# A head's values as high and low parts in one stationary block of the attention stages

## The reference

```python
# layer 0: 16 heads of 32, causal
q, k, v = ((x @ W.T).reshape(B, T, 16, 32).transpose(0, 2, 1, 3) for W in (Wq, Wk, Wv))
w = softmax(einsum('bhtd,bhsd->bhts', q, k) / sqrt(32) + mask)
z = einsum('bhts,bhsd->bhtd', w, v)
out = z.transpose(0, 2, 1, 3).reshape(B, T, 512) @ Wo.T
# layer 1: 32 query heads of 64 in 8 groups (4 query heads share one k and one v), causal
y = rms_norm(x) ; q, k, v = split(y @ w_in.T) ; q, k = rope(q), rope(k)
attn = softmax(where(causal, einsum('bghsd,bgxpd->bghsp', q, k) * 64 ** -0.5, -inf))
o = einsum('bghsp,bgxpd->bghsd', attn, v)
out = x + o.transpose(0, 3, 1, 2, 4).reshape(B, T, 2048) @ w_out.T
```

## Time and profile before

| | us |
|---|---|
| median of 3 runs | 2130.75 |
| the three runs | 2122.9, 2130.75, 2133.69 |
| the profiled execution | 2136.04 |
| its span, first to last instruction | 2134.7 |

### The profile page before, as it was taken

The page is one execution under the profiler, slowest core; times in us unless marked ns, Lnnn a source line. Parts: engine busy times, 40 slices in busy tenths (PEclk is TensorE's granted clock), DMA queues, the critical chain, the costliest instruction groups (busy, mean ns, idle before and its releaser), DMA issues. The chain is left out here.

```text
span 2134.7 us, 30662 instructions
## 1 busy us (share of the span) xinstructions
PE 1889.3 (89%) x10274; PEld 1632.2 (76%) x10274; DVE 1129.9 (53%) x2767; ACT 788.8 (37%) x2029; POOL 967.3 (45%) x926
## 2 busy tenths in 40 slices
PE   5788979878999999899569999999998999897896
PEld 4676867657899898799447888888877788785795
DVE  4555685437333333235746666666665656455344
ACT  2554643231222222121146556565553423212231
POOL 2332341248782759813736546455453101006584
PEclk8899999999999999899789999999999999789998
DMA  2434531025663446431533333233321110002565
GB/s 88 134 110 137 159 135 67 1 88 203 230 203 120 154 161 220 157 118 51 157 77 91 85 85 101 60 89 83 79 66 46 60 45 1 20 1 96 174 205 195
DMA packets 102630, 232.33 MB, mean 109 GB/s; under 512 B 18752, under 2 KB 19008, under 8 KB 99408
## 3 DMA queue, kind: packets, MB, share of 16 engines
q1 hardware_dynamic: 82736, 144.89, 22.8%
q0 software_dynamic: 19744, 85.47, 12.1%
HBM read 126.23 MB, written 57.93 MB: 86 GB/s over the span
## 5 line engine op out<-in xcount | busy, mean ns | idle before, releaser
L631 POOL TENSOR_SCALAR a_E<-a_E,a_inv 128x128 f32<-128x128 f32 (+3 forms) x384 | 218.9, 588 | 278.1 <-DVE a_inv L752 278.1
L149 PE MATMUL bank<-f_UH,f_XH 128*128 x596 | 202.2, 339 | 19.8 <-POOL f_UL L161 14.8
L664 ACT ACTIVATE a_E<-a_E,a_top 128x512 f32<-128x512 f32 (+3 forms) x384 | 211.1, 567 | 8.4 <-DVE a_top L746 8.3
L746 DVE CUSTOM_DVE_ANT_0 a_E<-a_causal,bank 128x512 f32<-128x512 bf16 (+3 forms) x384 | 164.2, 482 | 73.3 <-PE bank L897 45.9
L149 PE MATMUL bank<-f_UH,f_XL 128*128 x596 | 194.6, 327 | 0.0
L149 PE MATMUL bank<-f_UL,f_XH 128*128 x596 | 194.6, 326 | 0.0
L656 ACT ACTIVATE a_PHL<-bank 128x512 fp32r<-128x512 f32 (+1 forms) x288 | 131.2, 528 | 156.0 <-PE bank L913 156.0
L149 PE MATMUL bank<-a_PHL,a_VH 128*128 128x512 f32 (+3 forms) x768 | 186.7, 332 | 0.3 <-DVE a_QL L161 0.3
L161 DVE TENSOR_TENSOR a_PHL<-bank,a_PHL 128x512 fp32r<-128x512 f32 (+1 forms) x288 | 153.8, 587 | 29.7 <-ACT a_PHL L656 29.6
L1603 DVE TENSOR_TENSOR f_gate<-bank,f_gate 128x352 f32<-128x352 f32 x79 | 41.3, 523 | 215.9 <-PE bank L149 215.9
L149 PEld LDWEIGHTS bank<-a_PHL,a_VH 128*128 128x128 f32 x768 | 140.3, 196 | 16.3 <-DVE a_QL L161 0.6
(11 more groups left out here) (389 smaller groups left out, 4976.2 us busy)
## 6 DMA issues: line engine op xcount, KB each, us to landing
f_uraw<-f_up POOLq DMA_DIRECT2D x18, 1408.0 KB, 6.5
f_xb<-table SPq DMA_DIRECT2D x86, 256.0 KB, 3.1
table<-f_ob SPq DMA_DIRECT2D x86, 256.0 KB, 2.3
table<-a_zeros SPq DMA_DIRECT2D x31, 512.0 KB, 4.3
f_draw<-f_down POOLq DMA_DIRECT2D x27, 512.0 KB, 4.5
a_g<-a_f SPq DMA_DIRECT2D x160, 64.0 KB, 2.0
a_raw<-a_qkv SPq DMA_DIRECT2D x36, 256.0 KB, 3.1
f_uraw<-f_up POOLq DMA_DIRECT2D x9, 704.0 KB, 4.8
```

Of the source, the lines that this page charges most:

```text
L149: m = pe.matmul(out, a, b, start=first and i == 0 and j == 0, stop=last and i == n - 1 and j == 2, skip_group_check=not check)
L631: e.tensor_scalar(self.E[sl][:, a], self.E[sl][:, a], self.inv[:, sl, i:i + 1], 0.0, ALU.mult, ALU.add).then_inc(*self.s_nrm.up(N, m - 1, i))
L664: x = e.activation(E, E, ACT.Exp, scale=-1.0, bias=self.top[:, sl, i:i + 1], accum_out=self.total[:, sl, i:i + 1])
L746: e.tensor_tensor_reduce(self.E[sl][:, self.E_AT[i]:self.E_AT[i] + w], self.causal[:, T - w:T], bank[:, off:off + w], -1.0, HUGE, ALU.add, ...
```

## The change

- One block `V` of 128 x 128 per head and key tile takes the place of `VH` and `VL`: the high parts stay in the head's own columns, the low parts go to the columns 64 further on, modulo 128 (`across`).
- A job's weighted values are two matmuls for each key block and no longer three: `V` by the high weights and `V` by the low weights. The head's own rows get the high values' sum, the rows across get the low values' sum.
- Because the rows across are in use, only half of the heads share an accumulation (`half`): one head in a1, two in a0. So `bank[7]` is read out after every job in a1 (before: every second), and after every second job in a0 (before: every fourth), and the next group's first matmul waits for that readout.
- A readout is now: ScalarE copies 64 rows to `QH`; VectorE subtracts (64 rows), waits for its own result, and adds the rows across (`_dve_low_rows`).
- GpSimd clears one `V` in a0 and nothing of it in a1 (before: `VH` and `VL` in both).

```diff
@@ __init__
-        self.VH, self.VL = sb("VH", [heads, NT, P], F32R), sb("VL", [heads, NT, P], F32R)
+        self.V = sb("V", [heads, NT, P], F32R)
...
+        self.across = [slice((h * hd + P // 2) % P, (h * hd + P // 2) % P + hd) for h in range(heads)]
+        self.half = heads // 2
+        self.rows = [slice(0, P // 2), slice(P // 2, P)]
@@ pool
-        for z in (self.VH, self.VL):
-            e.memset(z[:, :, :, :].bitcast(F32), 0.0)
+        if self.heads > 2:
+            e.memset(self.V[:, :, :, :].bitcast(F32), 0.0)
@@ act
-            if 3 <= m < self.M + 3 and self.jobs[m - 3][3] == self.heads - 1:
+            if 3 <= m < self.M + 3 and self.jobs[m - 3][3] % self.half == self.half - 1:
                 j, b, r, h = self.jobs[m - 3]
+                own = self.rows[h // self.half]
                 e.wait_ge(*self.s_av.after(N, m - 3))
-                e.activation(self.QH[:, r, b * T:b * T + T], self.k.bank[self.OB][:, :], ACT.Copy).then_inc(
-                    *self.s_ohi.up(N, j, r, b))
+                e.activation(self.QH[own, r, b * T:b * T + T], self.k.bank[self.OB][own, :], ACT.Copy).then_inc(
+                    *self.s_ohi.up(N, j, r, b, h // self.half))
@@ dve
-            if 3 <= m < self.M + 3 and self.jobs[m - 3][3] == self.heads - 1:
...
+            if 3 <= m < self.M + 3 and self.jobs[m - 3][3] % self.half == self.half - 1:
+                self._dve_low_rows(*self.jobs[m - 3])
+
+    def _dve_low_rows(self, j, b, r, h):
+        e, N, g, bank = self.k.dve, self.name, h // self.half, self.k.bank[self.OB]
+        own, other = self.rows[g], self.rows[1 - g]
+        low = self.QL[own, r, b * T:b * T + T]
+        e.wait_ge(*self.s_ohi.after(N, j, r, b, g))
+        low_part(e, low, bank[own, :], self.QH[own, r, b * T:b * T + T]).then_inc(*self.k.d.up())
+        e.wait_ge(*self.k.d.now())
+        e.tensor_tensor(low, bank[other, :], low.bitcast(F32), ALU.add).then_inc(*self.s_olo.up(N, j, r, b, g))
@@ _dve_fill
-                    i = low_part(e, self.VL[:, h, bs, cs], src[:, :, cs], self.VH[:, h, bs, cs], scale=1.0)
+                    i = low_part(e, self.V[:, h, bs, self.across[h]], src[:, :, cs], self.V[:, h, bs, cs], scale=1.0)
@@ _pe_values
-        if h == 0 and self.OB in emptied:
+        first, last = h % self.half == 0, h % self.half == self.half - 1
+        if first and self.OB in emptied:
             e.wait_ge(*emptied[self.OB])
...
-                t = product(e, self.k.bank[self.OB][:, sblk * P:T],
-                            [(self.VH[:, h, b * TT + sblk, :], self.VL[:, h, b * TT + sblk, :])],
-                            [(self.PH[m % 2][:, a], self.PL[m % 2][:, a])],
-                            first=h == 0 and sblk == 0, last=h == self.heads - 1 and ci == 2)
+                e.matmul(out, self.V[:, h, at, :], self.PH[m % 2][:, a], start=first and sblk == 0, stop=False)
+                t = e.matmul(out, self.V[:, h, at, :], self.PL[m % 2][:, a], start=False, stop=last and ci == 2)
...
-        if h == self.heads - 1:
-            emptied[self.OB] = self.s_olo.after(N, j, r, b)
+        if last:
+            emptied[self.OB] = self.s_olo.after(N, j, r, b, h // self.half)
```

More of the change, by code:

```diff
@@ L531, in plan @@
                 self.s_av.plan((N, m))
-                if h == self.heads - 1:
-                    self.s_ohi.plan((N, j, r, b))
-                    self.s_olo.plan((N, j, r, b))
+                if h % self.half == self.half - 1:
+                    self.s_ohi.plan((N, j, r, b, h // self.half))
+                    self.s_olo.plan((N, j, r, b, h // self.half))
     def moves(self, j, c, b):
@@ L706, in _act_fill @@
                 e.wait_ge(*self.s_vt.after(N, j, b))
+                bs = slice(b * TT, b * TT + TT)
                 for h, cs in self.head_rows:
-                    i = e.activation(self.VH[:, h, b * TT:b * TT + TT, cs], src[:, :, cs], ACT.Copy, scale=1.0)
+                    i = e.activation(self.V[:, h, bs, cs], src[:, :, cs], ACT.Copy, scale=1.0)
                 i.then_inc(*self.s_vhi.up(N, j, b))
@@ L769, in dve @@
                 self.norm.dve_rest(NT + m)
-            if 3 <= m < self.M + 3 and self.jobs[m - 3][3] == self.heads - 1:
-                j, b, r, h = self.jobs[m - 3]
-                a = slice(b * T, b * T + T)
-                e.wait_ge(*self.s_ohi.after(N, j, r, b))
-                low_part(e, self.QL[:, r, a], self.k.bank[self.OB][:, :], self.QH[:, r, a]).then_inc(
-                    *self.s_olo.up(N, j, r, b))
+            if 3 <= m < self.M + 3 and self.jobs[m - 3][3] % self.half == self.half - 1:
[8 more added lines that the diff above has]
+        e.tensor_tensor(low, bank[other, :], low.bitcast(F32), ALU.add).then_inc(*self.s_olo.up(N, j, r, b, g))
     def _dve_rotate(self, x):
@@ L870, in _pe_fill @@
                 if g % TT == 0:
-                    e.wait_ge(*self.s_olo.after(N, j, self.queries[-1], g // TT))
+                    e.wait_ge(*self.s_olo.after(N, j, self.queries[-1], g // TT, 1))
                 a = slice(g * P, g * P + P)
@@ L928, in _pe_values @@
             for sblk, _ in chunk:
-                a = slice(self.P_AT[sblk], self.P_AT[sblk] + T - sblk * P)
-                t = product(e, self.k.bank[self.OB][:, sblk * P:T],
-                            [(self.VH[:, h, b * TT + sblk, :], self.VL[:, h, b * TT + sblk, :])],
-                            [(self.PH[m % 2][:, a], self.PL[m % 2][:, a])],
-                            first=h == 0 and sblk == 0, last=h == self.heads - 1 and ci == 2)
+                a, at = slice(self.P_AT[sblk], self.P_AT[sblk] + T - sblk * P), b * TT + sblk
+                out = self.k.bank[self.OB][:, sblk * P:T]
+                e.matmul(out, self.V[:, h, at, :], self.PH[m % 2][:, a], start=first and sblk == 0, stop=False)
+                t = e.matmul(out, self.V[:, h, at, :], self.PL[m % 2][:, a], start=False, stop=last and ci == 2)
         t.then_inc(*self.s_av.up(N, m))
-        if h == self.heads - 1:
-            emptied[self.OB] = self.s_olo.after(N, j, r, b)
+        if last:
+            emptied[self.OB] = self.s_olo.after(N, j, r, b, h // self.half)
     def end(self):
```

## The result

The changed kernel is slower by 0.7%: ratio 1.0071, 95% interval 1.0052 to 1.009; the medians of 10 runs each are 2144.15 us and 2127.03. The forecast was 2123. The profiled execution took 2146.57 us for 2136.04.

A forecast was written before the change was run, and what follows sets the result against it. Latency chains through ScalarE, SP, GpSimd and VectorE were taken to bound part of a1, TensorE the rest. a1 +2.6 and a0 -10.5 gave -7.9 us: 2128.1 profiled, 2123 median, 8-in-10 range 2104 to 2143.

The forecast's parts named there:

- The third pass: Values of each job: one of three passes saved, 0.63 us; 40 us in a1 and 20 in a0 if all on the path.
- a1, the stretch that TensorE sets: From B to the next projection before A: three V blocks saved and a small stall given back, -2.14 us per 8 jobs.
- B: Second of two a1 loops in eight (at 1376.96) beginning with scores waiting for stacking copies; wait 1.56 us, expected some 3.1.
- a1, loops without one before: a1 loops that had no readout: mask shifts about 1.7 us, hidden by VectorE's 1.94 us idle time at A, others similar.
- A: First of two a1 loops in eight (at 1360.84) beginning with scores waiting for stacking copies; wait 0.83 us, expected some 2.4.
- The clock: Longer waits drop TensorE's clock at B in all 8 groups instead of 4, 1.6 us each: +6.4 us in a1.
- a1, end: Last jobs of a1, without fill: each waits for the readout before it; +3.1 us, bounds -3.8 and +7.
- a1, start: Start of a1: GpSimd's two clearings go, so the norm on VectorE is faster; -1.5 us, bounds 0 and -2.9.
- a0: Stage a0: V blocks saved in loops that TensorE sets, little lost in the four end loops without fill; -10.5 us.
- VectorE becomes the bound: a1 loops without an earlier readout: shift over 1.94 us makes the rotation's first step late; +26 us, 2149 us, chance 0.16.
- Lighter chains: Sum of the rows across costs only 0.35 us, shortening chains before A and B, clock stays high: 2111 us, chance 0.20.
- "clock": Rival: all growing waits, one in a0 too, drop TensorE's clock; 6.4 us more, 2129 us, chance 0.15.

The follow-up runs named there:

- the copy first everywhere: Changed kernel with ScalarE's copy of the finished block ahead of its evacuation of a projection in all of a1: ratio 1.0057, a1 606.7 us.
- the waits filled: Changed kernel with identity matmuls on TensorE ahead of the scores' waits, 6 at A and 13 at B: ratio 1.0111, a1 613.6 us.
- the pass without its price: Kernel before, in a1 without the low values by high weights pass, still one readout per two jobs: ratio 0.9931, a1 571.6 us.

## Why the prediction was wrong

In the terms of the profiled execution I had -7.9 us and it was +10.5 (between the medians +17.1, of which the traces show only the 10.5). By its steps:

- **The third pass** was sized right (TensorE's loops without a wait went from 7.07 to 6.43 us, 0.64) and so was **the sum's own time** (0.69).
- **"a1, the stretch that TensorE sets"**: this step failed. I had -2.14 per 8 jobs for the way from B to the next projection, and +0.8 for the clock. Measured: the two loops behind B +0.69, the one after them -0.61, together +0.08 in the place of -1.34. The first two were not TensorE's. The output products in the second of them wait for the last readout of the batch, and this readout, its copy behind ScalarE's evacuation and its sum, sets them. I had read TensorE's unbroken row there as its own pace and had not followed who was next to be late. Three runs show it: without the sum the two loops fell by 1.3 us, with the copy first everywhere by 1.0, and with the waits filled they ended where they did in the groups where the clock stayed full.
- **"a1, loops without one before"**: the cover held at A, where the rotation's first step still found 1.46 us of idle time (1363.78), but I called the other loops alike, and in 15 of 21 it was used up (the waits before that step fell from 23.4 us to 4.4 in 6). **A to B** therefore grew by 1.37 and not 0.73. **Up to A** it was +0.45 where I had +0.73.
- Together 8 jobs took +1.90 us where I had +0.12: over the six full groups 10.7 us, the largest part of the miss.
- **The clock**: it fell behind every B, as I said (0.69 or 0.79 in the loop behind it), but the 1.6 us each were mis-sized, and five groups had a drop before, not four (the first, at 1113 us, too). I had compared the first loop alone. With the one behind it, the kernel before took 8.79 + 9.74 = 18.53 us with a drop and 7.18 + 10.09 = 17.27 without: 1.3. In the changed kernel the drop at B costs nothing, as the slow loop loses waiting time that the next one would have had. Where it costs is where nothing waits behind it, in the second loop of the filled kernel and at the end of a1, and there I had no term. The rule of the Trainium skill that I had cited ("TensorE: Matmul & The Clock Gate", section "HAM oscillation — how this bites in real kernels") told the drops at B rightly, not the time.
- **"a1, end"**: +7.2 for +3.1, at the upper bound I had named. The last two waits, 2.12 and 2.22 us, came as I had walked them (2.1, and 0.8 more than 1.50). The wait of 1.04 I had as -0.1, and 1.4 of the miss is the clock in the output products.
- **"a1, start"**: -1.3 for -1.5, which is luck in part, as the same start took 42.15, 42.15 and 44.62 us in the three runs of the changed a1. **a0**: -8.4 for -10.5, right in kind; up to job 28 it was 14.0 ahead, and its loops without fill gave 5.6 back where I had 0.4.
- The other 4 us are scatter of the stages between.

The rival "VectorE becomes the bound" named the time (2149), the lost cover and the late first step, and had 0.16. Its place was wrong: not the loop at A, but those at and behind B. What speaks against it in its pure form is that VectorE is idle for 21% of the middle of a1: it is late in a chain, and not full. "Lighter chains" was out with the 688 ns of the sum, "clock" as the price at B with the filled waits.

## What to carry to other kernels

A loop in which an engine never waits is not yet a loop that it sets: before taking work off it, find the next wait it would run into, and who ends that one. An operation added to an engine that works in order costs its time once in every chain that passes over it (0.69 us, some four times in eight loops), and its input's place in another engine's order counts too (5 us of a1). A drop of the clock is priced by the loop behind it as well: where that one ended in a wait the drop was free here, where it didn't it was paid. When a pass can be bought off the busiest engine for work on the others, first see what the same engine's waits are worth: here a low part moved by one loop took 22.6 us from a1 (585.9 to 563.3), and the pass without its price 14.3.

## What the runs showed of the hardware

- VectorE's product of two SBUF tiles takes 0.69 us when it starts first and 1.78 when GpSimd's product, which reads SBUF too, began 0.47 us ahead of it; GpSimd's takes 1.29 us alone and 1.80 as the second:

```profile
1363.78 0.69 DVE L794 TENSOR_TENSOR a_f<-a_f,a_cos_sin 128x512 f32<-128x512 f32 x1 [1.46 <-DMA a_g<-a_f]
1372.07 1.78 DVE L794 TENSOR_TENSOR a_f<-a_f,a_cos_sin 128x512 f32<-128x512 f32 x1
```

```profile
1363.83 1.80 POOL L628 TENSOR_TENSOR a_g<-a_g,a_cos_sin 128x512 f32<-128x512 f32 x1 [8.22 <-DMA a_g<-a_f]
1371.60 1.71 POOL L628 TENSOR_TENSOR a_g<-a_g,a_cos_sin 128x512 f32<-128x512 f32 x1 [3.50 <-DMA a_g<-a_f]
```

  The Trainium skill says so ("SBUF — State Buffer", section "Who interferes with whom"): a VectorE instruction with two SBUF inputs contends with a GpSimd instruction that reads SBUF. By that rule I could have told the stretched first step from the lost cover beforehand.
- Filling an idle time of 3.2 us with matmuls that compute nothing kept the granted clock at 1.00 in all seven loops behind the filled waits at B, where it had been 0.68 to 0.79. In five of the seven it fell one loop later instead, to 0.77 or 0.88.
- An operation on 64 rows of a bank took 688 ns, like one on 128 (0.69), also where its inputs came from the other half of the rows.
